# A graph network on one core: setup reordered, softmax shared with GpSimd, weights stored in two parts

## The reference

```python
h = jnp.maximum(_layernorm(x, axis=-1), 0.0)
x = x + _L0_gnn_ref(h, src, dst, ...)      # attention, 8 heads of 16
h = jnp.maximum(_layernorm(x, axis=-1), 0.0)
x = x + _L1_gnn_ref(h, edge_attr_16, ...)  # four layers of gated messages
h = jnp.maximum(_layernorm(x, axis=-1), 0.0)
x = x + _L2_gnn_ref(h, edge_index, ...)    # two convolutions
h = jnp.maximum(_layernorm(x, axis=-1), 0.0)
x = x + _L3_gnn_ref(h, edge_index, ...)    # one linear sum
```

```python
score = jnp.einsum('ehd,ehd->eh', q[dst], k[src]) * rel_pri / SQRT_DK
smax = jax.ops.segment_max(score, dst, num_segments=N)
e = jnp.exp(score - smax[dst])
ssum = jax.ops.segment_sum(e, dst, num_segments=N)
t = jax.ops.segment_sum(v[src] * (e / ssum[dst])[:, :, None], dst, num_segments=N).reshape(N, DIM)
new_h = (t @ Wa + ba) * alpha + h * (1.0 - alpha)      # alpha = sigmoid(skip)
```

## Time and profile before

| | us |
|---|---|
| median of 3 runs | 10655.52 (10635.86 to 10660.82) |
| the profiled execution, its own time | 10607.1 |
| its span | 10605.0 |
| VectorE busy | 3028.2 (29%) |
| GpSimd busy | 6216.3 (59%) |
| TensorE matrix products busy | 5675.4 (54%) |
| ScalarE busy | 949.0 (9%) |

### The profile page before, as it was taken

The page is one execution under the profiler, slowest core; times in us unless marked ns, Lnnn a source line. Parts: engine busy times, 40 slices in busy tenths (PEclk is TensorE's granted clock), DMA queues, the critical chain, the costliest instruction groups (busy, mean ns, idle before and its releaser), DMA issues.

```text
span 10605.0 us, 107124 instructions
## 1 busy us (share of the span) xinstructions
PE 5675.4 (54%) x23750; PEld 3922.0 (37%) x23751; DVE 3028.2 (29%) x7366; ACT 949.0 (9%) x1767; POOL 6216.3 (59%) x6738
## 2 busy tenths in 40 slices
PE   3566637566775667656675666653334333333334
PEld 2333437333443334433343333333333333333234
DVE  3444577212221122312222122331122112231222
ACT  1111100111111111101111111110000000000000
POOL 3655536565555655466554655546666666656665
PEclk7566659777887788878788778875566556665666
DMA  5777755332323323233332323221111111111111
GB/s 167 218 219 218 203 139 155 90 88 82 85 75 86 87 82 85 79 85 87 83 83 75 88 81 81 77 59 45 47 49 48 46 46 49 48 46 46 47 49 47
DMA packets 796948, 945.08 MB, mean 89 GB/s; under 512 B 269045, under 2 KB 530448, under 8 KB 796302
## 3 DMA queue, kind: packets, MB, share of 16 engines
q0 software_dynamic: 213408, 463.35, 16.4%
q1 hardware_dynamic: 474970, 390.60, 13.2%
q10 hardware_dynamic: 108436, 89.99, 2.6%
HBM read 797.55 MB, written 152.25 MB: 90 GB/s over the span
## 4 chain that ended last, share of the span: by engine, by line
another core or an unknown queue 44%; PE 18%; issue 13%; DVE 9%; DVEq 3%; POOL 0%; SPq 0%; ACT 0%; DMA 0%; ACTq 0%; POOLq 0%
PE ps_big L1119 8%; PE ps_seg L1126 5%; DVE onehots L1715 2%; DVE sums L1746 2%; DVEq L453 1%; PE ps_seg L1197 1%; PE ps_big L1197 1%; PE ps_big L1063 1%; PE ps_t L1038 1%; DVE gate L1894 1%; DVE h_res L1898 0%; DVE group_stats L1783 0%; PE ps_seg L1063 0%; PE ps_big L987 0%
## 5 line engine op out<-in xcount | busy, mean ns | idle before, releaser
L871 POOL DMA_INDIRECT rows<-node_rows,idx_all x5488 | 5209.8, 949 | 3470.5 <-SPq L713 1590.0
L1119 PE MATMUL ps_big<-rows,ident 128*128 (+1 forms) x1960 | 1221.8, 709 | 1386.0 <-DVE onehots L1715 1249.5
L1746 DVE TENSOR_TENSOR sums<-sums,ps_seg 128x128 f32 x1342 | 385.5, 287 | 5141.3 <-remote 3368.8
L1126 PEld LDWEIGHTS ps_seg<-onehots 128*128 128x128 f32 x7840 | 1206.0, 223 | 899.0 <-issue 735.5
L1126 PE MATMUL ps_seg<-onehots 128*128 128x128 f32 x7840 | 1236.4, 309 | 260.6 <-issue 168.0
L1715 DVE SCALAR_TENSOR_TENSOR onehots<-ps_mm,away 128x512 f32<-128x512 f32 x1975 | 1349.3, 684 | 21.4 <-issue 13.8
L1197 PE MATMUL ps_seg<-rows,onehots 128*128 (+1 forms) x2952 | 613.8, 372 | 1235.4 <-DVE onehots L1715 595.8
L1119 PE MATMUL ps_big<-q_res,ident 128*128 (+1 forms) x1960 | 1153.9, 674 | 150.9 <-issue 123.0
L1119 PEld LDWEIGHTS ps_big<-rows,ident 128*128 128x128 f32 x1960 | 412.0, 224 | 2036.2 <-DVE onehots L1715 1461.7
L871 POOL DMA_INDIRECT sums<-kv_rows,idx_all x784 | 743.4, 948 | 548.2 <-SPq L711 281.2
L1197 PEld LDWEIGHTS ps_seg<-rows,onehots 128*128 128x128 f32 x2952 | 536.7, 272 | 1301.7 <-DVE onehots L1715 619.0
(11 more groups left out here) (215 smaller groups left out, 2974.4 us busy)
## 6 DMA issues: line engine op xcount, KB each, us to landing
q_res<-gates_by_edge SPq DMA_DIRECT2D x784, 256.0 KB
rows<-node_rows,idx_all POOLq DMA_INDIRECT x5488
rows<-dst_padded SPq DMA_DIRECT2D x196, 256.0 KB
value_rows_by_edge<-sums SPq DMA_DIRECT2D x196, 256.0 KB
gates_by_edge<-gate ACTq DMA_DIRECT2D x196, 256.0 KB
rows<-value_rows_by_edge SPq DMA_DIRECT2D x196, 256.0 KB, 3.5
node_rows<-h_res ACTq DMA_DIRECT2D x49, 448.0 KB
sums<-kv_rows,idx_all POOLq DMA_INDIRECT x784
```

The source lines that it names most:

```text
L871: pool.indirect_dma_start(target[:, r, j, :], None, table, bass.IndirectOffsetOnAxis(ap=idx_all[:, c * J + j:c * J + j + 1], axis=0), elem ...
L1119: last = nc.tensor.matmul(ps_big[u][:, :], ident[:, :], chunk_words(source, slot, 0, CHUNK), start=n == 0, stop=n == 1)
L1126: last = nc.tensor.matmul(ps_seg[u][:, 0:D], onehots[:, u, j, :], msg[:, u, j, 0:D], start=j == 0, stop=j == J - 1)
L1746: V.tensor_tensor(mine, mine, seg_four[(n - 1) % depth][:, 0:D], ALU.add).then_inc(agg_added, 1)
```

## The change

In the setup the 49 statistics are written out, with one semaphore increment at the end instead of one each; the same for the aggregates. SP issues the neighbour loads ahead of its parameter loads, once the padded indices are stored. VectorE does the order check between statistics and aggregates, and the fused weights ahead of the table of steps; TensorE's order follows. The clear of `tab_d[1]` is gone from the setup; SP stores `h_res` there instead, after it has issued the load of `away`, in the softmax.

In the softmax VectorE does the two maxima of each head and counts them in `carried`; GpSimd does the subtractions, and ahead of them the skip term of groups 3 to 6, each in three operations (multiply, add the bias, add to x), from the moment VectorE has finished its own three. SP stores the weights of the first 10 partitions (`FIRST_PARTS`, those of chunks 0 to 13), issues the seven value loads, then the store of the other 118 partitions, waits for the first store alone, and loads the weights of chunks 0 to 6 and 7 to 13. It waits for the second store before it loads those of chunks 14 to 20.

```diff
@@ -367,6 +371,8 @@
         GROUPS = WINDOWS // GROUP
+        EARLY = 3
+        FIRST_PARTS = -(-2 * RING * CHUNK // FLAT)
...
@@ -389,6 +395,11 @@
+        by_edge = lambda a: a.rearrange("p (i h) -> p i h", h=HEADS)
+        by_head = lambda a: a.rearrange("p (h i) -> p i h", h=HEADS)
+        score_e = by_edge(score[:, :, :].rearrange("p c k -> p (c k)"))
+        a_e, a_h, b_h = by_edge(scan_a), by_head(scan_a), by_head(scan_b)
...
             sp.wait_ge(padded, 1)
             sp.dma_start(src_d.rearrange("(p i) -> p i", p=P), src_flat[:, :]).then_inc(padded_stored, 16)
             sp.dma_start(dst_d.rearrange("(p i) -> p i", p=P), dst_flat[:, :]).then_inc(padded_stored, 16)
+            sp.wait_ge(padded_stored, 32)
+            flat_rows = dst_d.rearrange("(p i) -> p i", p=P)
+            sp.dma_start(edge_nb[1:P, 0:1], flat_rows[0:P - 1, FLAT - 1:FLAT]).then_inc(nb_loaded, 16)
+            sp.dma_start(edge_nb[0:P - 1, 1:2], flat_rows[1:P, 0:1]).then_inc(nb_loaded, 16)
             sp.wait_ge(consts_made, 2)
             for dst, src in loads_once()[:FIRST_LOADS]:
                 sp.dma_start(dst, src).then_inc(params_loaded, 16)
-            sp.wait_ge(padded_stored, 32)
-            sp.wait_ge(consts_made, 3)
-            flat_rows = dst_d.rearrange("(p i) -> p i", p=P)
-            sp.dma_start(edge_nb[1:P, 0:1], flat_rows[0:P - 1, FLAT - 1:FLAT]).then_inc(nb_loaded, 16)
-            sp.dma_start(edge_nb[0:P - 1, 1:2], flat_rows[1:P, 0:1]).then_inc(nb_loaded, 16)
             with if_unsorted(sp, "sp"):
...
             sp.wait_ge(words_made, 1)
             sp.dma_start(words_d.rearrange("f (g p) -> p f g", p=P), word[:, :, :]).then_inc(words_stored, 16)
-            sp.dma_start(tab_d[1].rearrange("(p w) d -> p (w d)", p=P),
...
                         else:
                             wait_alone(sp, "sp", read_sem, freed[early + r] + read_base)
                         fill(turn * RING + r, r)
+                        if kind == "values" and r == 0 and isinstance(turn, int) and turn == 1:
+                            sp.wait_ge(weights_stored, 16)
                         if kind == "values" and r == 0 and more:
                             load_weights(turn + 1, 1 - half)
...
-            sp.wait_ge(table_cleared, 16)
             chunk_pass(0, "scores", products_made, 0, also=load_words)
...
@@ -774,15 +781,22 @@
             sp.wait_ge(away_stored, 16)
             sp.dma_start(away[:, :].rearrange("p (s j) -> p s j", j=J),
                          away_d[BEFORE:BEFORE + LAST + 4, :].rearrange("s (p j) -> p s j", j=J)).then_inc(away_loaded, 16)
+            sp.dma_start(tab_d[1].rearrange("(p w) d -> p (w d)", p=P), h_res[:, :, :].rearrange("p w d -> p (w d)"))\
+                .then_inc(table_cleared, 16)
+            sp.wait_ge(table_cleared, 16)
             sp.wait_ge(exp_ready, HEADS)
-            sp.dma_start(flat(weight_d), scan_a).then_inc(weights_stored, 16)
-            sp.wait_ge(weights_stored, 16)
+            sp.dma_start(flat(weight_d)[0:FIRST_PARTS, :], scan_a[0:FIRST_PARTS, :]).then_inc(weights_begun, 16)
+            def store_weights():
+                sp.dma_start(flat(weight_d)[FIRST_PARTS:P, :], scan_a[FIRST_PARTS:P, :]).then_inc(weights_stored, 16)
+                sp.wait_ge(weights_begun, 16)
+                load_weights(0, 0)
+                load_weights(1, 1)
             def load_weights(turn, half):
                 sp.dma_start(score[:, ds(turn * RING, RING), :], by_chunk(weight_d)[:, ds(turn * RING, RING), :])\
                     .then_inc(weights_loaded[half], 16)
-            load_weights(0, 0)
-            chunk_pass(1, "values", segsum_ready, 0, also=lambda: load_weights(1, 1))
+            chunk_pass(1, "values", segsum_ready, 0, also=store_weights)
...
@@ -898,7 +912,20 @@
                 pool.indirect_dma_start(away_rows[:, g, :], None, dst_d.rearrange("(c e) -> c e", e=CHUNK),
                                         bass.IndirectOffsetOnAxis(ap=chunk_of[:, g:g + 1], axis=0)).then_inc(away_fetched, 16)
-            wait_alone(pool, "pool", weights_loaded[0], 16)
+            behind = Chain(pool, pool_chain)
+            pool.wait_ge(skip_begun, 1)
+            G = nc.gpsimd
+            for g in range(EARLY, GROUPS):
+                seven = slice(g * GROUP, (g + 1) * GROUP)
+                behind(G.tensor_scalar(group_y[:, :, :], h_res[:, seven, :], alpha[:, 1:2], None, ALU.mult))
+                behind(G.tensor_tensor(out=group_y[:, :, :], in0=group_y[:, :, :],
+                                       in1=b_out[:, :].rearrange("p (a d) -> p a d", a=1).to_broadcast([P, GROUP, D]), op=ALU.add))
+                behind(G.tensor_tensor(out=x_res[:, seven, :], in0=x_res[:, seven, :], in1=group_y[:, :, :], op=ALU.add))
+            for h in range(HEADS):
+                pool.wait_ge(carried, h + 1)
+                G.tensor_tensor(out=a_e[:, :, h], in0=score_e[:, :, h], in1=b_h[:, :, h], op=ALU.subtract).then_inc(shifted, 1)
...
@@ -943,10 +970,6 @@
                     nc.tensor.matmul(ps_mm[1][:, 1:2], ones_row[:, :], sort_run[:, FLAT - 1:FLAT], start=True, stop=True)\
                         .then_inc(sort_summed, 1)
-            pe.wait_ge(lasts_made, 1)
-            nc.tensor.matmul(ps_mm[0][:, 0:CHUNKS], ones_row[0:1, :], last_step[0:1, :],
-                             start=True, stop=True).then_inc(lasts_spread, 1)
...
+            pe.wait_ge(lasts_made, 1)
+            nc.tensor.matmul(ps_mm[0][:, 0:CHUNKS], ones_row[0:1, :], last_step[0:1, :],
+                             start=True, stop=True).then_inc(lasts_spread, 1)
             pe.wait_ge(w_ready, 1)
...
             dve.wait_ge(cleared, 1)
             dve.wait_ge(x_loaded, 32)
-            with dve.Fori(0, WINDOWS) as w:
-                V.bn_stats(stats[:, ds(w, 1), :].rearrange("p w d -> p (w d)"),
-                           x_res[:, ds(w, 1), :].rearrange("p w d -> p (w d)")).then_inc(stats_made, 1)
-            dve.wait_ge(stats_made, WINDOWS)
             for w in range(WINDOWS):
-                V.bn_aggr(mv[:, w, :], stats[:, w, :]).then_inc(stats_made, 1)
-            dve.wait_ge(stats_made, 2 * WINDOWS)
-            inverse_root(chain, rstd[:, :], mv[:, :, 1], EPS, root_all[:, 0, :], root_all[:, 1, :])
-            V.scalar_tensor_tensor(nmr[:, :], mv[:, :, 0], -1.0, rstd[:, :], ALU.mult, ALU.mult).then_inc(ln_ready, 1)
+                last = V.bn_stats(stats[:, w, :], x_res[:, w, :])
+            last.then_inc(stats_made, 1)
             dve.wait_ge(padded, 1)
             dve.wait_ge(nb_loaded, 32)
             chain(V.tensor_tensor(sort_run[:, 1:FLAT], dst_flat[:, 0:FLAT - 1], dst_flat[:, 1:FLAT], ALU.is_gt))
             chain(V.tensor_tensor(sort_run[:, 0:1], edge_nb[:, 0:1], dst_flat[:, 0:1], ALU.is_gt))
             chain(V.tensor_reduce(sort_small[:, 0:1], sort_run, AX.X, ALU.add))
             dve.sem_inc(order_counted, 1)
+            dve.wait_ge(stats_made, 1)
+            for w in range(WINDOWS):
+                last = V.bn_aggr(mv[:, w, :], stats[:, w, :])
+            last.then_inc(stats_made, 1)
             dve.wait_ge(order_summed, 1)
             V.tensor_copy(unsorted[:, :], ps_mm[1][0:1, 0:1]).then_inc(order_known, 1)
+            dve.wait_ge(stats_made, 2)
+            inverse_root(chain, rstd[:, :], mv[:, :, 1], EPS, root_all[:, 0, :], root_all[:, 1, :])
+            V.scalar_tensor_tensor(nmr[:, :], mv[:, :, 0], -1.0, rstd[:, :], ALU.mult, ALU.mult).then_inc(ln_ready, 1)
             with if_unsorted(dve, "dve"):
...
                     dve.sem_inc(sort_ready, 1)
+            dve.wait_ge(params_loaded, 16 * len(loads_once()))
+            chain(V.tensor_scalar(pri[:, :], pri[:, :], float(DK) ** -0.5, None, ALU.mult))
...
+            dve.wait_ge(alpha_made, 1)
+            chain(V.tensor_scalar(alpha[:, 1:2], alpha[:, 0:1], -1.0, 1.0, ALU.mult, ALU.add))
+            chain(V.tensor_scalar(b_out[:, :], b_out[:, :], alpha[:, 0:1], None, ALU.mult))
             dve.wait_ge(lasts_loaded, 16)
...
             add_skip(0, EARLY)
+            dve.sem_inc(skip_begun, 1)
             dve.wait_ge(scores_flat, 16)
...
             chain(scan(a_h, same_prev, score_e, False))
-            chain(scan(b_e, same_next, a_h, True))
-            V.tensor_copy(ends[:, 0, :], b_e[:, FLAT - 1, :])
-            V.tensor_copy(ends[:, 2, :], b_e[:, 0, :]).then_inc(ends_ready, 1)
+            chain(scan(b_h, same_next, a_h, True))
+            V.tensor_copy(ends[:, 0, :], b_h[:, FLAT - 1, :])
+            V.tensor_copy(ends[:, 2, :], b_h[:, 0, :]).then_inc(ends_ready, 1)
             dve.wait_ge(ends_turned, 1)
...
@@ -1700,12 +1715,9 @@
             dve.wait_ge(ends_turned, 2)
             chain(V.tensor_copy(carry[:, :, :].rearrange("p n h -> p (n h)"), ps_mm[1][:, 0:2 * HEADS]))
             for h in range(HEADS):
-                chain(V.scalar_tensor_tensor(b_e[:, :, h], from_left, carry[:, 0, h:h + 1], b_e[:, :, h], ALU.add, ALU.max))
```

(30 more changed lines are left out.)

21 lines of the change are left out of this document (1 added, 20 removed).

## The result

The changed kernel took 10696.22 us, the kernel before 10644.32 in the same comparison (medians of five runs each). The ratio is 1.0055, 95% interval 1.0036 to 1.0074: 59 us slower (38 to 79). Forecast were +68 us (range +10 to +90, chance of slower 0.74). The forecast of 10724 us stood on a median of 10655.5 us; that the median of before is 11 us lower here makes up 11 of the 28 us between forecast and measurement.

The account below looks back on a forecast made before the run. GpSimd, busy 59% of the span mostly issuing gathers the change leaves alone, was taken as the bound. Setup -6, softmax +22, store +53 and slots -1 gave +68 us on a 10655.5 us median: 10724 us, range 10665 to 10745.

Parts of the forecast that it names:

- Statistics worth nothing: Setup: writing out the statistics saves VectorE 13.8 us, but it then waits for neighbour loads landing at about 45 us.
- my terms, 54 + 5 + 10.6: Setup: root or parameter loads done by 54 us, then weights some 5 us and the table some 10.6 us.
- Clear removed, -6.6 us, not 18.6: Setup: without the table clear the key/value stores' stall ends 6.6 us earlier, since the step words still take 12.1 us.
- Setup: Whole setup: -6.6 + 0.7 = -6 us, range -13 to 0.
- Scans, +16.4 us: Softmax scans: VectorE waits 16.4 us for GpSimd's twelve skip operations, as the two engines exclude each other.
- Heads 4.29 us, +5.7 us: Softmax maxima: each head takes 4.29 us instead of 3.60 because GpSimd's subtraction blocks VectorE; +5.7 us.
- Softmax in all: Softmax: scans and heads together, +22 us.
- 118 rows on two engines, first weighing at 66 us: Weights' store: 59 rows on each of two engines take 55.5 us; first weighing 66 us after the exponentials, +53 us.
- Seven full slots, -1 us: Weighted sum: with seven slots full, the first seven chunks go at about 1.16 us rather than 1.25; -1 us.
- Rival B: Two engines for the store but little exclusion between GpSimd and VectorE, softmax -8 us; +38 us in all, chance 0.17.
- C: Rival: second store part spread over all 16 engines, with exclusion; store +5 us, +20 us in all, chance 0.15.
- D: Rival: all 16 engines, no exclusion, neighbour loads landing at once; -17 us in all, chance 0.08.

Follow-up runs that it names:

- e10: e9 with ScalarE issuing the edge-attribute copy only after the parameter and neighbour loads; measured -8 us (-20 to 3) against the kernel before.
- e2: The kernel before with only the two-part weights' store added (10 rows, then 118 behind the seven value loads); measured +73 us (54 to 93) against it.
- e1: The changed kernel with the weights' store split into 16 + 112 rows instead of 10 + 118; measured +13 us (2 to 23) against the kernel before.
- e4: The changed kernel with the four skip groups and eight subtractions back on VectorE; measured +37 us (21 to 53) against the kernel before.
- e11: e10 with the last-node load also ahead of parameters and copy, and ScalarE storing the 112 rows; measured -21 us (-33 to -8) against the kernel before.
- e12: The changed kernel with GpSimd's twelve skip operations cut to three of every seven windows; measured +54 us against the kernel before, one run.
- e5: The changed kernel with the weights' store split into 15 + 113 rows; measured +100 us against the kernel before, one run.
- e7: The changed kernel with GpSimd's twelve skip operations moved behind its eight subtractions; measured +47 us (23 to 73) against the kernel before.
- e6: The changed kernel with the weights' store split into 11 + 117 rows; measured +26 us against the kernel before, one run.
- e9: The changed kernel with softmax work on VectorE, 16 + 112 rows stored, weight loads ahead of value loads; measured +1 us (-9 to 12) against the kernel before.

## Why the prediction held, step by step

- **Statistics worth nothing, VectorE idle to 45 for the neighbour loads.** Idle to 44.18; table at 70.2 (69.8 forecast; my terms, 54 + 5 + 10.6, make 69.6). That the attribute copy is the cause was argued; e10 shows it: 19.03 us of holding became 1.02.
- **Clear removed, -6.6 us, not 18.6.** From the issue of the step words to the end of the stall it is 12.8 us (78.45 to 91.26), 19.5 before (77.65 to 97.15): 6.7 less. As the table came 1.0 us later, the stall ended 5.9 us earlier. No run takes out the clear alone. Setup -5.5 to the first gather; forecast -6.
- **Scans, +16.4 us.** 17.4 with the copies behind them. Here two wrong sizes cancelled. I had a skip group at 4.5 us of GpSimd; it is 6.9 (2.53 + 2.08 + 2.08 and gaps). And I let VectorE wait for nearly all of the price (16.4 of 18 us), where it waits 17.4 / 12 = 1.45 us an operation, some two thirds of it. With the right price and my share of it the term would have been 25 us, 8 too many: that it came out is luck. (The two prices that I worked from give 1.82 us for 896 elements, and not the 1.7 to 1.8 that I took.) The rule I used, that the work adds up, holds for some two thirds of GpSimd's time; which part of an operation that is, no run shows.
- **Heads 4.29 us, +5.7 us.** 3.86 us, +2.4. The subtraction was priced well (2.4 forecast, 2.23 alone), but it blocks a maximum for 2.87 - 1.03 = 1.84 us and not for 2.15. Softmax in all +19.9, forecast +22.
- **118 rows on two engines, first weighing at 66 us.** 67.8, and 66.9 in e2; 0.917 us a row against 0.94. +55 against +53.
- **Seven full slots, -1 us.** The pace is there: a chunk every 1.17 us (1615.70, 1616.87, 1618.04). The gain is not, for the stretch behind grew by 2.0 us.
- **The sum.** The direction and the stage that decides it are as forecast. The stages give +71 us and the medians +59 (38 to 79); both hold the forecast of +68. Rival B (+38) lies at the edge of the interval, and its mechanism is refuted by the scans. C and D fall with the 118 rows; C's arithmetic is what e1 shows (forecast +20, stages +25, measured +13).

The Trainium skill's rule for the number of engines ("DMA: Bandwidth & Descriptors", section "Why a DMA increments its semaphore by 16 and not by 1") would put 112, 113, 117 and 118 rows on 16, 1, 13 and 2 engines; the line through the four times agrees, and so do the shares of 0.84, 0.14 and 0.08 for 117, 118 and 113. Its page "SBUF — State Buffer" (section "Who interferes with whom") says that a VectorE operation with two SBUF inputs contends with a GpSimd one that reads SBUF. The trace agrees, scans included. Its section "Summary: rules for kernel authors" lets the second of the two wait until the first finishes; here the maximum issued at 1537.25 ends at 1540.12, so with 1.03 us of its own it began at about 1539.1, 0.2 us before the subtraction's end at 1539.30, and beside the scans VectorE waits 1.45 us on average for operations of 2.08 to 2.53. So by the trace VectorE goes on before GpSimd's operation has ended; only the copy of 8 columns waited to its end.

What stays open: the rest of the program behind the first gather of the next pass took 8682 us in the profile of before and 8709 in the changed one, between 8662 and 8695 in the kernels of e1 to e4, e11 and e12, and between 8590 and 8623 in those of e5 to e10, whose two comparisons had the kernel before at 10519 to 10521 us, some 95 us faster. Within these groups there is no order by edit. I take it for scatter; nothing here shows another cause.

## What to carry to other kernels

Count the rows of each part before splitting a store: 118 rows ran on two DMA engines and 113 on one, for no larger number up to 16 divides them, and 10 + 118 rows cost 55 us where 16 + 112 cost 8. Moving work to GpSimd beside two-input VectorE operations saved nothing here, even in scans: it cost 17.3 us for the skip groups and 2.5 for the subtractions. Put it where VectorE has no such work and where GpSimd itself has the time. When a small load waits behind a bulk copy, moving it uncovers the next small load, so move all of them ahead, and hold the copy until they have landed.

## What I had not expected of the hardware

- GpSimd's one-input form with a scalar of each partition is slower than its two-input forms: 2.53 against 2.08 us for 896 elements, with no such VectorE operation beside it (e7).
- Issuing a load behind a store on few engines can hold the issuing queue itself: SP stood 47.49 us over two weight loads behind 118 rows, 92.31 us behind 113, and 2.19 us (e6) behind 117.
- A VectorE copy with one input waits for GpSimd as well: 1.85 us instead of 0.17, to within 0.03 us of the end of GpSimd's addition.
- A store of 16 rows takes 5.2 us with the engines to itself (e9) and 8.1 beside one of 112 rows from another queue (e11).
